# Context attention in a four-layer decoder: the rows of the next sequence are normed one group of heads before the group that transposes them

## The chip, the cores and the metric

The kernel runs on one core of one Trainium2 chip. The metric is the device time of one execution in microseconds (us), read as the median of several runs. The engines are TensorE (PE, its weight loads as PEld), VectorE (DVE), ScalarE (ACT), GpSimd (POOL) and SyncE (SP), each with its own stream of instructions that it works off in order.

## What is computed

A decoder of four layers on x, 8 sequences of 112 rows of 256 numbers, with a context of 8 x 375 rows of 128 numbers. Each layer is an attention, an attention over the context ("xattn") and a feed-forward part, each added to x after a layer norm of its input. The change touches three of these parts. The one of layer 3 is the shortest:

```python
x = x + _L3_xattn_ref(_layernorm(x, axis=-1), ctx_512, L3_xattn_Wq, L3_xattn_Wkv, L3_xattn_Wo)

def _L3_xattn_ref(x, z, Wq, Wkv, Wo):
    Q = (x @ Wq.T).reshape(B, xN, NUM_HEADS, HEAD_DIM)          # 16 heads of 16
    KV = (z @ Wkv.T).reshape(B, zN, 2, NUM_HEADS, HEAD_DIM)
    attn = softmax(einsum('bqhd,bkhd->bhqk', Q, K) * SCALE)
    O = einsum('bhqk,bkhd->bqhd', attn, V).reshape(B, xN, DIM)
    return O @ Wo.T
```

Layer 1's is the same with biases. Layer 2's second block (`a2_...` weights) has 16 heads of 32, norms its input twice, norms the context too, and has a GELU part behind it.

## The kernel before

`build` runs twelve stages one after the other, and a stage opens only when all engines have closed the one before. The three stages of the change are `Cross(k, "l1x")` (layer 1, about 788 to 957 us of the profile), `L2Block2` (about 1456 to 1667 us) and `CrossL3` (about 2080 to 2252 us), all of the class `Tiled` (L828).

**One order for all engines.** `Tiled.order` (L856) yields steps (kind, sequence b, index), and every engine's function walks through the same list and issues its own share of each step. So a step's place in the list sets its place in the stream of every engine that has a share in it. A sequence's 16 heads go in four groups of four, g = 0 to 3. Iteration (b, g) yields, in this order:

- `four` of the next group: 4 score products on PE, one into each of the banks 0 to 3 (L908); DVE takes the row maxima in two halves (L994). PE waits first until all four exponentials of the group before have left the banks (L905);
- `turn4` (g, 0), then `low` and `high` of the next group (ACT, 4 exponentials with their sums, L956), then `turn4` (g, 1): PE transposes the weights of this group (L917, by the helper at L264), ACT copies the first third (L978) and DVE the two others (L1002);
- `values4` of the group before (PE, L934), `turn4` (g, 2);
- then the list `plan[g]`: small steps for the sequence b + ahead. `stats` is a chain of four instructions on DVE (`bn_stats` L785, memset L787, `bn_aggr` L788, L790), with one power on POOL (L811) for the inverse deviation; `xn` is DVE's subtract and multiply of the 112 x 256 rows (L795), which waits for that power; `xT` is two transposes on PE (L548, by L264), which wait for `xn`, and DVE's copy (L798; L2231 in layer 2); `q`, `k`, `v`, `vv` are the projections (PE by L259), `inverse` the transposed reciprocal sums (PE, and ACT L984), `y` the output projection;
- after group 0, `norm` of the sequence before (DVE L1015).

In layer 2 `plan[0]` goes on behind `xT` with `cstat` (DVE, statistics of the context, L2378 to L2386), `v` 2 and `cn` (POOL, L2398 and L2405), and the context's transpose `cT` in group 1 waits for `cn`. There `ln` and `xm` make the rows that `xn` reads.

There is one buffer `xn`, one `xT` and one set of row statistics, `k.stats`. Transposes and projections take their banks in turn from a ring of three (4, 5, 7); a product waits until the bank's last reader is done (`fill`, L243). The context of each sequence comes by a DMA on SP's queue.

Of the kernel before, what the change touches and what calls it, by code (L numbers as in the profile page):

```python
# [827 lines left out]
class Tiled(Attention):  # L828
# [11 lines left out]
    second = ()  # L840
# [1047 lines left out]
class Cross(Tiled):  # L1888
# [1 line left out]
    hd = 16  # L1890
    scale, k_pieces, qm = 0.25, KD, None
    prologue = (("stats", 0), ("xn", 0), ("k", 0), ("xT", 0), ("parity", 0), ("q", 0))
    second = (("k", 1, 0), ("vv", 0, 0), ("v", 2, 0), ("stats", 0, 1))
    plan = ((("inverse", 0, -1), ("xn", 0, 1), ("xT", 0, 1)),
            (("q", 0, 1), ("k", 0, 1)),
            (("y", 0, -1), ("k", 1, 1)),
            (("vv", 0, 1), ("stats", 0, 2), ("v", 2, 1)))
    epilogue = (("y", 0),)

    def __init__(self, k, pack):  # L1900
# [72 lines left out]
class L1Attn(TiledSelf):  # L1973
# [3 lines left out]
    second = (("v", 0, 0), ("stats", 0, 1), ("xn", 0, 1), ("xT", 0, 1))  # L1977
    plan = ((("k", 0, 1),), (("q", 0, 1), ("near", 0, 0)), (("v", 0, 1), ("stats", 0, 2)), (("xn", 0, 2),),
            (("xT", 0, 2), ("y", 0, 0)))
# [304 lines left out]
class L2Block1(L2Block, TiledSelf):  # L2284
    k_pieces, key_step, v_by_act = 1, 4, (0,)
    lib, ln, ln3 = 4, 0, 8
    prologue = (("ln", 0), ("xm", 0), ("stats", 0), ("xn", 0), ("xT", 0), ("k", 0), ("q", 0))
    second = (("v", 0, 0), ("ln", 0, 1), ("xm", 0, 1), ("stats", 0, 1), ("xn", 0, 1), ("xT", 0, 1))
    plan = ((("k", 0, 1), ("xn3", 0, -1), ("ln", 0, 2)), (("q", 0, 1), ("xm", 0, 2)),
            (("v", 0, 1), ("xT3", 0, -1), ("stats", 0, 2)), (("xn", 0, 2),), (("xT", 0, 2), ("y", 0, 0), ("stats3", 0, 0)))  # L2290
# [27 lines left out]
class L2Block2(L2Block, Tiled):  # L2318
    k_pieces, v_by_act = 4, (0, 1, 2)
    lib, ln, ln3 = 6, 2, 16  # L2320
    prologue = (("ln", 0), ("xm", 0), ("cstat", 0), ("stats", 0), ("cn", 0), ("xn", 0), ("xT", 0), ("q", 0), ("cT", 0),
                ("k", 0), ("k", 1))
    second = (("k", 2, 0), ("v", 0, 0), ("v", 1, 0), ("ln", 0, 1), ("xm", 0, 1), ("stats", 0, 1))
    plan = ((("inverse", 0, -1), ("xn", 0, 1), ("xT", 0, 1), ("cstat", 0, 1), ("v", 2, 0), ("cn", 0, 1)),
# [3 lines left out]
    epilogue = (("y", 0), ("stats3", 0), ("xn3", 0), ("xT3", 0))  # L2328

    def __init__(self, k):  # L2330
# [1352 lines left out]
```

## Time and profile before

| what | value |
|---|---|
| median of 3 runs (lowest, highest) | 2377.60 us (2376.21, 2378.54) |
| span of the profiled execution | 2376.3 us |
| busy: PE, DVE, ACT, POOL | 2041.1, 1355.0, 884.5, 502.1 us |
| PE's share of the chain of waits that ended last | 66% |
| mean clock granted to PE | 0.857 of full speed |

The profile is one execution, and for that one only the span, first to last instruction, is given; it lies inside the three runs, 1.3 us below their median. Busy times are of the whole program; the three stages of the change take about a quarter of it. In a timeline a row gives the start, the duration, the engine, the line, what is written and read, how many instructions are merged, and in brackets the idle time before it with the one that ended it. "End" below is start plus duration.

### The profile page before, as it was taken

What the parts mean: (1) busy time and instruction counts of PE and PEld (TensorE: products, weight loads), DVE (VectorE), ACT (ScalarE), POOL (GpSimd) and SP (SyncE); (2) the same over time, 40 slices, a digit from 0 to 9 for tenths busy, and PEclk for the clock granted to TensorE, in tenths of its full rate; (3) what the DMA queues carried; (4) which work ended last, traced back from release to release, by engine and by line L of the source; (5) the groups of instructions that cost most, each with busy time, mean ns of one, the idle gap of its engine ahead of it and who ended that gap; (6) DMA issues with size and microseconds to landing.
All of it is one profiled execution on the core that took longest, in us unless ns stands there. A gap on an engine that the chain in (4) does not pass through costs nothing.

```text
span 2376.3 us, 57229 instructions
## 1 busy us (share of the span) xinstructions
PE 2041.1 (86%) x22720; PEld 1482.7 (62%) x22720; DVE 1355.0 (57%) x3605; ACT 884.5 (37%) x3421; POOL 502.1 (21%) x1131
## 2 busy tenths in 40 slices
PE   7999999998978799897977887999999998889843
PEld 3788888786656566466865654666554544556522
DVE  5666666674345688544634723787263210678797
ACT  2344444353236566211324522665111111246511
POOL 3344444221001100101324512332000000401111
PEclk9655555799988899998998998999899999789956
DMA  3000000104000000300021000000030000000000
GB/s 133 4 5 4 5 4 5 74 2 177 1 1 1 14 11 5 133 1 23 1 80 47 2 1 10 8 8 5 1 147 0 1 0 1 1 14 15 2 0 16
DMA packets 7752, 57.20 MB, mean 24 GB/s; under 512 B 760, under 2 KB 5216, under 8 KB 5728
## 3 DMA queue, kind: packets, MB, share of 16 engines
q1 hardware_dynamic: 7488, 53.54, 5.9%
q8 instruction: 183, 3.00, 0.5%
q14 instruction: 81, 0.66, 0.1%
HBM read 52.62 MB, written 0.92 MB: 23 GB/s over the span
## 4 chain that ended last, share of the span: by engine, by line
PE 66%; DVE 16%; issue 9%; ACT 5%; POOL 4%; DMA 1%; DVEq 0%; POOLq 0%; ACTq 0%; SPq 0%
PE banks L259 42%; PE banks L264 8%; PE banks L1323 6%; PE banks L908 3%; DVE memory L1421 2%; PE banks L934 2%; ACT memory L1352 1%; PE banks L1474 1%; ACT memory L1359 1%; DVE memory L795 1%; DVE memory L1218 1%; DVE memory L1427 1%; DVE memory L1430 1%; DVE memory L1439 1%; DVE memory L994 1%
## 5 line engine op out<-in xcount | busy, mean ns | idle before, releaser
L259 PE MATMUL banks<-memory 128*112 128x256 f32 (+7 forms) x4192 | 1130.1, 426 | 68.9 <-POOL memory L2030 8.0
L259 PEld LDWEIGHTS banks<-memory 128*128 128x128 f32 (+3 forms) x4192 | 706.7, 196 | 396.3 <-issue 250.6
L264 PE MATMUL banks<-memory 112*125 112x112 f32 (+3 forms) x2000 | 309.8, 288 | 151.0 <-DVE memory L795 92.0
L264 PEld LDWEIGHTS banks<-memory 112*125 112x125 f32 (+3 forms) x2000 | 240.3, 173 | 270.0 <-issue 139.4
L1323 PE MATMUL banks<-memory 128*128 128x8 bf16 (+2 forms) x10752 | 325.8, 175 | 25.9 <-DVE memory L1439 5.8
L1323 PEld LDWEIGHTS banks<-memory 128*128 128x128 bf16 x10752 | 304.0, 104 | 48.3 <-DVE memory L1439 46.2
L956 ACT ACTIVATE memory<-banks,memory 112x375 f32<-112x375 f32 x384 | 215.4, 579 | 26.2 <-DVE memory L994 26.0
L994 DVE TENSOR_REDUCE memory<-banks 112x2 f32<-112x750 f32 x192 | 171.1, 934 | 45.4 <-PE banks L908 43.7
L1002 DVE COPY memory<-banks 125x448 f32<-125x448 f32 x192 | 116.6, 619 | 12.8 <-PE banks L264 8.7
L1421 DVE TENSOR_REDUCE memory<-banks 128x48 f32<-128x192 f32 x448 | 109.6, 286 | 5.5 <-PE banks L1323 5.5
L1502 ACT ACTIVATE memory<-memory 112x112 f32<-112x112 f32 x192 | 71.7, 375 | 86.2 <-DVE memory L1523 86.2
L811 POOL TENSOR_TENSOR memory<-memory 112x1 f32<-112x1 f32 x72 | 39.7, 551 | 299.2 <-DVE memory L790 297.7
L1352 ACT ACTIVATE memory<-memory 128x48 f32<-128x48 f32 x224 | 54.4, 243 | 128.0 <-DVE memory L1421 128.0
L978 ACT COPY memory<-banks 125x448 f32<-125x448 f32 x96 | 51.1, 533 | 130.6 <-PE banks L264 130.6
L908 PE MATMUL banks<-memory 32*112 32x375 f32 x768 | 89.0, 533 | 8.6 <-ACT memory L956 6.3
L3142 DVE TENSOR_TENSOR memory<-banks,memory 112x256 f32<-112x256 f32 x8 | 3.4, 425 | 158.4 <-PE banks L259 158.4
L1383 POOL TENSOR_TENSOR memory<-memory 128x16 f32<-128x16 f32 x224 | 48.6, 217 | 205.7 <-DVE memory L1439 205.7
L1201 ACT ACTIVATE memory<-banks,memory 112x112 f32<-112x112 f32 x256 | 86.4, 391 | 9.7 <-DVE memory L1218 8.2
L1366 ACT COPY banks<-memory 128x48 f32<-128x48 f32 x448 | 79.8, 178 | 23.7 <-DVE memory L1400 23.7
L3119 ACT ACTIVATE memory<-banks,memory 128x448 f32<-128x448 f32 x32 | 20.3, 635 | 173.5 <-PE banks L259 173.5
L1439 DVE SCALAR_TENSOR_TENSOR memory<-memory 128x16 f32<-128x16 f32 x224 | 39.2, 175 | 75.7 <-ACT memory L1359 75.7
L956 ACT ACTIVATION_READ_ACCUMULATOR memory<-banks,memory 112x1 f32 x384 | 80.6, 210 | 0.0
(233 smaller groups left out, 2404.1 us busy)
## 6 DMA issues: line engine op xcount, KB each, us to landing
memory<-in_l2x SPq DMA_DIRECT2D x1, 7680.0 KB, 21.5
memory<-in_l2f SPq DMA_DIRECT2D x1, 7168.0 KB, 19.6
memory<-in_l1f SPq DMA_DIRECT2D x1, 4617.0 KB, 15.9
memory<-in_ctxT SPq DMA_DIRECT2D x24, 187.5 KB
memory<-in_l0a SPq DMA_DIRECT2D x1, 4224.0 KB, 16.1
memory<-in_l2f SPq DMA_DIRECT2D x1, 4096.0 KB, 12.9
memory<-in_l3f SPq DMA_DIRECT2D x1, 3073.0 KB, 22.4
memory<-in_l2a SPq DMA_DIRECT2D x1, 3072.0 KB, 19.2
```

Of the source, the lines that this page charges most:

```text
L259: ins = self.nc.tensor.matmul(out, weights[i], acts[i], start=i == 0, stop=i == n - 1)
L264: return self.nc.tensor.transpose(out, in_, self.ident[0:n, 0:n])
L908: ins = PE.matmul(k.bank(bank, S, CK), q, kT, start=True, stop=True)
L956: self.nc.scalar.activation(self.P_both[gi % 2][:, r, :], self.k.bank(r, S, CK), ACT.Exp, bias=u["nmax"][:, 4 * i + r:4 * i + r + 1], scal ...
L994: V.tensor_reduce(u["nmax"][:, 4 * i + 2 * h:4 * i + 2 * h + 2], k.banks[0:S, 2 * h:2 * h + 2, 0:CK], AX, ALU.max, negate=True).then_inc(* ...
L1002: V.tensor_copy(self.PT_both[gi % 2][0:CR, c, :], k.bank(k.at["turn", gi, c], CR, 4 * S)).then_inc(*s.pt_v.up())
L1201: A.activation(self.P_all[:, i, g, :], k.bank(i, S, 4 * S)[:, g * S:(g + 1) * S], ACT.Exp, bias=u["nmax"][:, 4 * i + g:4 * i + g + 1], sca ...
L1323: ins = self.nc.tensor.matmul(own[:, part:3, at:at + B], whh[:, part, l, j, g * P:(g + 1) * P], self.upper[l][:, 0:3 - part, j * B:(j + 1) ...
L1352: A.activation(self.gates[:, l, 1:4, :].rearrange("p g c -> p (g c)"), self.sums[:, l, 0:6 * B], ACT.Tanh).then_inc(*s.act_tanh.up())
L1366: self.nc.scalar.copy(self.slots[l][last][:, 3, :], src).then_inc(*self.s.xw_in.up())
L1421: V.tensor_reduce(self.sums[:, l, first * B:end * B], self.slots[l][last].rearrange("p s c -> p c s"), AX, ALU.add).then_inc(*s.gates_in.up())
L1502: A.activation(weights, weights, ACT.Exp, bias=self.nmax[n % 2][:, at:at + 1], scale=1.0, accum_out=self.total[n % 2][:, at:at + 1]).then_ ...
```

## The change

Two tables are rewritten, the `plan` and `second` of `Cross` (which `CrossL3` inherits) and of `L2Block2`. In `Cross`, `stats` of sequence b + 2 moves from group 3 to the end of group 2 of iteration b, and `xn` of the same sequence from group 0 of the next sequence to the end of group 3, behind `v`. In `L2Block2` `stats` stays and `xn` moves in the same way, behind `xT3` and `v` 1. In `second`, the steps between the first two groups of scores, `xn` of sequence 1 is put last, and in `Cross` `stats` of sequence 1 is put ahead of the value projections. Nothing is added or taken out.

```diff
 class Cross(Tiled):
-    second = (("k", 1, 0), ("vv", 0, 0), ("v", 2, 0), ("stats", 0, 1))
-    plan = ((("inverse", 0, -1), ("xn", 0, 1), ("xT", 0, 1)),
+    second = (("k", 1, 0), ("stats", 0, 1), ("vv", 0, 0), ("v", 2, 0), ("xn", 0, 1))
+    plan = ((("inverse", 0, -1), ("xT", 0, 1)),
             (("q", 0, 1), ("k", 0, 1)),
-            (("y", 0, -1), ("k", 1, 1)),
-            (("vv", 0, 1), ("stats", 0, 2), ("v", 2, 1)))
+            (("y", 0, -1), ("k", 1, 1), ("stats", 0, 2)),
+            (("vv", 0, 1), ("v", 2, 1), ("xn", 0, 2)))
 class L2Block2(L2Block, Tiled):
-    second = (("k", 2, 0), ("v", 0, 0), ("v", 1, 0), ("ln", 0, 1), ("xm", 0, 1), ("stats", 0, 1))
+    second = (("k", 2, 0), ("v", 0, 0), ("v", 1, 0), ("ln", 0, 1), ("xm", 0, 1), ("stats", 0, 1), ("xn", 0, 1))
-    plan = ((("inverse", 0, -1), ("xn", 0, 1), ("xT", 0, 1), ("cstat", 0, 1), ("v", 2, 0), ("cn", 0, 1)),
+    plan = ((("inverse", 0, -1), ("xT", 0, 1), ("cstat", 0, 1), ("v", 2, 0), ("cn", 0, 1)),
...
-            (("k", 2, 1), ("xn3", 0, -1), ("v", 0, 1), ("stats", 0, 2), ("xT3", 0, -1), ("v", 1, 1)))
+            (("k", 2, 1), ("xn3", 0, -1), ("v", 0, 1), ("stats", 0, 2), ("xT3", 0, -1), ("v", 1, 1), ("xn", 0, 2)))
```

The instructions of PE, ACT and SP keep their order; only DVE's and POOL's streams differ. This is DVE's in layer 1, from the output addition of a sequence (L779, L781, group 2) to the copy of the next sequence's turned rows (L798, group 0). Before:

```order
1546 L779 TENSOR_TENSOR memory<-banks,memory 112x256
1547 L781 TENSOR_TENSOR memory<-memory 112x256
1548 L994 TENSOR_REDUCE memory<-banks 112x2 x2
1549 L1002 COPY memory<-banks 125x448 x2
1550 L1007 RECIPROCAL memory<-memory 112x16
1551 L1094 TENSOR_TENSOR memory<-banks,memory 125x2x8x16 x2
1552 L785 BN_STATS memory<-memory 112x6
...
1556 L1080 TENSOR_TENSOR memory<-banks,memory 125x8x16 x2
1557 L994 TENSOR_REDUCE memory<-banks 112x2 x2
1558 L1002 COPY memory<-banks 125x448 x2
1559 L795 TENSOR_SCALAR memory<-memory 112x256
1560 L798 COPY memory<-banks 128x224
```

After:

```order
1546 L779 TENSOR_TENSOR memory<-banks,memory 112x256
1547 L781 TENSOR_TENSOR memory<-memory 112x256
1548 L785 BN_STATS memory<-memory 112x6
...
1552 L994 TENSOR_REDUCE memory<-banks 112x2 x2
1553 L1002 COPY memory<-banks 125x448 x2
1554 L1007 RECIPROCAL memory<-memory 112x16
1555 L1094 TENSOR_TENSOR memory<-banks,memory 125x2x8x16 x2
1556 L1080 TENSOR_TENSOR memory<-banks,memory 125x8x16 x2
1557 L795 TENSOR_SCALAR memory<-memory 112x256
1558 L994 TENSOR_REDUCE memory<-banks 112x2 x2
1559 L1002 COPY memory<-banks 125x448 x2
1560 L798 COPY memory<-banks 128x224
```

The four instructions of `stats` stand one group earlier, ahead of the maxima of the next sequence's group 0; the norm L795 stands ahead of the maxima of group 1 and of two copies, where it stood behind them. Layer 3 has the same order with other lines. In layer 2, on DVE, from the end of group 3 into group 0, this is the difference (minus is before, plus is the change; L2231 is first the copy of `xT3`, then that of `xT`):

```order
 L790 TENSOR_SCALAR memory<-memory 112x1
 L2231 TENSOR_SCALAR memory<-banks,memory 128x112 x2
-L994 TENSOR_REDUCE memory<-banks 112x2 x2
-L1002 COPY memory<-banks 125x448 x2
-L795 TENSOR_SCALAR memory<-memory 112x256
+L795 TENSOR_SCALAR memory<-memory 112x256
+L994 TENSOR_REDUCE memory<-banks 112x2 x2
+L1002 COPY memory<-banks 125x448 x2
 L2231 TENSOR_SCALAR memory<-banks,memory 128x112 x2
 L2378 BN_STATS memory<-memory 125x6 x3
```

Here only the norm moves, ahead of two maxima and two copies. On POOL, the power L811 of layers 1 and 3 now stands ahead of the copy L1034 (`share`) in each sequence, where it stood behind it; in layer 2 POOL's order is as before.

## Rows read from the trace of the kernel before

**Rows 1.** Who waited for whom, PE, whole span: total, times, longest.

```profile
PE banks L264 <- DVE memory L795: 92.0, 39, 9.9
```

**Rows 2.** PE's transposes (L264): idle before them ended by L795; layers 1, 2, 3.

```profile
  DVE memory L795: 9.8, 7
...
  DVE memory L795: 9.2, 8
...
  DVE memory L795: 9.9, 8
```

**Rows 3.** Timeline, layer 1, group 3 into group 0 of a middle sequence.

```profile
840.12 0.42 DVE L785 BATCH_NORM_STATS2 memory<-memory 112x6 f32<-112x256 f32 x1
...
840.87 0.49 DVE L1080 TENSOR_TENSOR memory<-banks,memory 125x128 f32<-125x128 f32 x2
...
841.27 1.77 DVE L994 TENSOR_REDUCE memory<-banks 112x2 f32<-112x750 f32 x2
...
842.24 0.57 ACT L956 ACTIVATE memory<-banks,memory 112x375 f32<-112x375 f32 x1 [0.38 <-DVE memory L994]
842.36 0.88 PE L264 MATMUL banks<-memory 112*125 112x112 f32 x6
...
844.02 0.41 DVE L795 TENSOR_SCALAR memory<-memory 112x256 f32<-112x256 f32 x1
844.35 0.21 ACT L956 ACTIVATION_READ_ACCUMULATOR memory<-banks,memory 112x1 f32 x1
...
844.48 0.41 PE L264 MATMUL banks<-memory 112*128 112x112 f32 x2 [1.24 <-DVE memory L795]
...
844.82 0.90 PE L908 MATMUL banks<-memory 32*112 32x375 f32 x8
```

**Rows 4.** The same timeline later: groups 1 to 3, scores and maxima.

```profile
849.58 0.90 PE L908 MATMUL banks<-memory 32*112 32x375 f32 x8
...
850.51 1.78 DVE L994 TENSOR_REDUCE memory<-banks 112x2 f32<-112x750 f32 x2 [0.66 <-PE banks L908]
...
855.22 1.78 DVE L994 TENSOR_REDUCE memory<-banks 112x2 f32<-112x750 f32 x2 [0.57 <-PE banks L908]
...
858.39 0.22 ACT L956 ACTIVATION_READ_ACCUMULATOR memory<-banks,memory 112x1 f32 x1
...
858.81 0.90 PE L908 MATMUL banks<-memory 32*112 32x375 f32 x8
```

**Rows 5.** Timeline, layer 3: maxima behind the output addition, and PE's wait.

```profile
2152.02 1.78 DVE L994 TENSOR_REDUCE memory<-banks 112x2 f32<-112x750 f32 x2 [1.04 <-PE banks L908]
...
2160.33 0.41 PE L264 MATMUL banks<-memory 112*128 112x112 f32 x2 [1.24 <-DVE memory L795]
```

**Rows 6.** Timeline, layer 2: group 3 into groups 0 and 1 of a middle sequence.

```profile
1520.96 0.55 POOL L811 TENSOR_TENSOR memory<-memory 112x1 f32<-112x1 f32 x1 [0.93 <-DVE memory L790]
...
1522.07 1.78 DVE L994 TENSOR_REDUCE memory<-banks 112x2 f32<-112x750 f32 x2 [0.58 <-PE banks L908]
...
1525.39 0.41 PE L264 MATMUL banks<-memory 112*128 112x112 f32 x2 [0.66 <-DVE memory L795]
...
1525.84 0.70 DVE L2231 TENSOR_SCALAR memory<-banks,memory 128x112 f32<-128x112 f32 x2 [0.51 <-PE banks L264]
...
1528.16 1.77 DVE L994 TENSOR_REDUCE memory<-banks 112x2 f32<-112x750 f32 x2
...
1531.14 0.54 PE L264 MATMUL banks<-memory 125*128 125x125 f32 x3 [0.60 <-POOL memory L2405]
```

**Rows 7.** Timeline, layer 2, first sequence: PE's longest wait for the norm.

```profile
1476.08 0.63 PE L264 MATMUL banks<-memory 112*128 112x112 f32 x2 [4.14 <-DVE memory L795]
```

**Rows 8.** Windows, layer 1: PE, PEld, DVE, ACT, POOL busy, granted clock, DMA share, GB/s.

```profile
900.00:902.00 2.00, 0.76 (x10) 0.41 (x9) 1.58 (x4) 1.96 (x8) 0.00 (x0) 1.00 0.19 68
902.00:904.00 2.00, 2.00 (x12) 0.93 (x12) 1.23 (x3) 0.00 (x0) 0.00 (x0) 0.54 0.00 0
```

**Rows 9.** Timeline, layer 1: `share` copies, one in each sequence.

```profile
877.51 0.40 POOL L1034 COPY memory<-memory 112x256 f32<-112x256 f32 x1 [16.90 <-DVE memory L1007]
896.56 0.40 POOL L1034 COPY memory<-memory 112x256 f32<-112x256 f32 x1 [16.89 <-DVE memory L1007]
917.19 0.40 POOL L1034 COPY memory<-memory 112x256 f32<-112x256 f32 x1 [18.47 <-DVE memory L1007]
```

**Rows 10.** Timeline, layer 3's prologue: a norm beside POOL's memsets.

```profile
2085.00 2.75 DVE L795 TENSOR_SCALAR memory<-memory 112x256 f32<-112x256 f32 x1 [0.73 <-POOL memory L811]
```

**Rows 11.** Windows as in rows 8: first sequences of layers 1, 3 and 2.

```profile
807.00:809.00 2.00, 2.00 (x29) 1.66 (x28) 1.66 (x3) 1.82 (x6) 0.00 (x0) 0.50 0.00 0
...
2104.00:2106.00 2.00, 2.00 (x28) 1.47 (x28) 1.47 (x3) 2.00 (x8) 0.00 (x0) 0.50 0.00 0
...
1476.00:1478.00 2.00, 1.92 (x4) 0.79 (x4) 1.27 (x6) 0.16 (x2) 0.00 (x0) 0.50 0.00 0
```

**Rows 12.** Timeline, layer 2: POOL's norm of the context.

```profile
1528.73 2.36 POOL L2405 TENSOR_SCALAR memory<-memory 125x128 f32<-125x128 f32 x3
```

**Rows 13.** Timeline, layer 1: `share` of the sequence of rows 3.

```profile
839.41 0.40 POOL L1034 COPY memory<-memory 112x256 f32<-112x256 f32 x1 [16.89 <-DVE memory L1007]
```

## The prediction

> **What bounds the kernel now.** I began with the list of who waited for whom on PE, since PE is busy 86% of the span and has two thirds of the chain that ended last. Its first line is the wait of the transposes (L264) for the norm L795: 92.0 us in 39 waits [rows 1]. That sum is of the whole program. Cut to the three stages that the change touches, it is 9.8, 9.2 and 9.9 us [rows 2], 28.9 us in all, and a few of these 23 waits stand in the prologues, which the change leaves alone. So the gain cannot reach 29 us, and most of the 92 us lie in stages without an edit.
>
> Next the timeline of a middle sequence of layer 1, to see what would end PE's idle time if the norm were there. PE is done with the last turn and the inverse at 842.36 + 0.88 = 843.24, stands 1.24 us, transposes the rows at 844.48 and starts the scores at 844.82 [rows 3]. But the scores have a second condition: the last exponential of the group before must have left its bank. It ends at 844.35 + 0.21 = 844.56 [rows 3], and where this condition alone held PE, PE began 0.20 us later (858.39 + 0.22 = 858.61, then 858.81) [rows 4]. So with the norm for nothing, the scores could start at 844.76 instead of 844.82. **The wait of 1.24 us hides another that ends 0.06 us earlier.** The exponentials began at 842.24, released by the maxima, and these began at 841.27 with no idle time before them: DVE was late [rows 3]. PE alone would let the maxima start 0.93 us after the scores, as at 849.58 and 850.51 [rows 4]. What the change is worth in layers 1 and 3 is therefore what it does to DVE's place of the maxima of group 1, not to the norm.
>
> **The change, part by part.**
>
> *Layer 1, a middle sequence (6 of them).* Out of the stretch ahead of the group 1 maxima goes `stats`, 840.87 - 840.12 = 0.75 us [rows 3]. In comes the norm, 0.41 us [rows 3]. An instruction of DVE can start a little before the one ahead has ended (L1080 ends at 840.87 + 0.49 = 841.36, the maxima start at 841.27 [rows 3]), so that 0.32 to 0.41 us of it count; I take 0.37. The maxima start 0.38 us earlier. The 0.75 us of `stats` go to the end of group 2, where DVE idles 0.57 us before the maxima of group 0 [rows 4]. So these start about 0.11 to 0.18 us later, and DVE has no idle time from there to the maxima of group 1. Net 0.20 to 0.27 us earlier; exponentials and the next scores follow by the same amount. The transposes themselves stop waiting for the norm: they now wait for DVE's first copy of the group, which frees their bank, and for nothing behind it. I take **0.25 us a sequence**, times 6 is 1.5 us. The bounds are 0.06 (the maxima do not move) and 1.24 (PE's whole wait).
>
> *Layer 3 (6 middle sequences).* PE's wait is the same 1.24 us, but the output addition is one instruction instead of two, and DVE idles 1.04 us before the group 0 maxima [rows 5]. That covers the 0.75 us of `stats` wholly; if this cover were gone, the case would be layer 1's. The full 0.38 us arrives, plus up to 0.06 of the hidden slack: **0.40 us**, times 6 is 2.4 us.
>
> *Layer 2 (6 middle sequences).* Here only the norm moves. It stands behind the power L811, which ends at 1520.96 + 0.55 = 1521.51 [rows 6], so it runs from about 1521.55 to 1521.95, and the maxima of group 1 began at 1522.07 after 0.58 us of idle time [rows 6]. It is covered, with 0.1 us to spare. In group 0 PE waited 0.66 us at the transposes [rows 6]; without it the rows' copy on DVE comes 0.65 us earlier than 1525.84, and behind it, with no gap, the context's statistics, `norm` and the maxima of group 2 at 1528.16 [rows 6]. So DVE's chain moves by the full amount, and with it POOL's `cn`, for which PE waits 0.60 us at 1531.14 [rows 6]: that wait stays, but ends earlier. I take **0.64 us**, times 6 is 3.8 us. The bounds are 0 (another wait takes all of it) and 0.66.
>
> *The first sequence of each stage.* In layers 1 and 3 `stats` of sequence 1 moves into time in which DVE waits for the value projections, and costs nothing; the norm takes its place ahead of the maxima. By the same 0.38 us the scores of group 2 come earlier: 0.8 us for both. In layer 2 DVE is held in `second` by the norm's wait for POOL's power (0.55 us) before it may take the maxima, a loss of about 1.1 us, but PE's wait of 4.14 us [rows 7] shrinks by more. I take a gain of 0.5 us, between -1 and +2.
>
> PE, ACT and SP keep their order, and the DMA of the context waits for the same steps as before. POOL's power now stands ahead of `share`, which waits for DVE much longer than the power takes: nothing. The sum is 1.5 + 2.4 + 3.8 + 0.8 + 0.5 = **9.0 us**.
>
> *The clock.* At 902 us the granted clock falls from 1.00 to 0.54 behind a window in which PE was busy 0.76 of 2 us [rows 8], that is to the lower of its levels of 2.4 and 1.2 GHz. The engine had just stood its 1.24 us. That sequence took 917.19 - 896.56 = 20.63 us, the one before 896.56 - 877.51 = 19.05 [rows 9], so the fall cost 1.58 us. One of six like waits brought it on; with the gap cut in two I expect none there. That gives 1.6 us, **10.6 us in all**. The first sequences of all three stages have such a stretch at the lower level too (0.50 from 807, from 2104 and from 1476 us) [rows 11], and I leave those as they are. The Trainium skill (TensorE: Matmul & The Clock Gate, Part 1) says that the monitor behind the clock runs freely and does not start with the kernel. By this rule a gap may or may not bring a fall, and the sum would stay at 9.0 us on average; the trace agrees so far that one of six like gaps did it.
>
> Against the profiled span this is 2376.3 - 10.6 = 2365.7 us. The span is 1.3 us under the median of the three runs, so for the median I predict 2377.6 - 10.6 = **2367 us**. A measurement of this kernel can tell about 0.2%, 4.8 us, from no change.
>
> **The rivals.**
>
> *The hidden wait keeps nearly all.* If the maxima of group 1 do not come earlier in layers 1 and 3, each of 14 sequences gains 0.06 us, 0.8 us in all. With layer 2's 4.3 us and no clock gained the sum is 5 us: 2372.5 us, on the bound of no change. For it speaks that ACT idles only 0.38 us before its first exponential at 842.24 [rows 3]: its copy L978 is next in line there, and had that been any later, nothing would move; against it that 0.38 us of DVE's work leave the stretch for certain. Chance 0.13.
>
> *PE's whole wait goes.* All of the waits for the norm outside the prologues vanish, about 27 us: 2350 us. The exponentials' end at 844.56 speaks against it. Chance 0.03.
>
> *The clock gives more.* The falls in the three first sequences go too, each about 1.6 us, 5 us more: 2362 us. For it speaks that layer 2's follows right on the wait of 4.14 us for the norm [rows 7]; against it that PE still waits there for the exponentials. Chance 0.17.
>
> *Slower: DVE is held by the norm behind POOL.* DVE works in order, so while the norm waits for the power, the maxima, both copies and `xT`'s copy wait too. In layer 2 the power comes 0.1 us before the norm is due. If POOL were busy then with `cn` (2.36 us [rows 12]) or the chain behind `xm`, the maxima would be late by up to 2 us in each of 7 sequences, 14 us less the 9 of the gain: 2383 us. It decides from 0.6 us of lateness on, where layer 2 gives nothing. Against it: POOL had idled 0.93 us before that power [rows 6]. Akin to it is the port: one norm took 2.75 us instead of 0.41 beside POOL's memsets [rows 10]. The Trainium skill (SBUF — State Buffer, Who interferes with whom) says that VectorE in a two-port mode and GpSimd lock each other out for a whole instruction; the row agrees. It would add at most the 0.4 us of `share` in layers 1 and 3, 12 times, 4.8 us: 2372 us. But `share` runs from 839.41 to 839.81 [rows 13], and the norm's new place is near 840.5. Chance of both together 0.05.
>
> **How the numbers follow.** My forecast has the rest, 0.62. Its own range is 2363 to 2371: each of the 0.25, 0.40 and 0.64 may be off by half, 4 us. The range goes to the clock case below, with two more such falls gained or lost by chance in the later program (3 us and more), and to the hidden wait above: **2358 to 2374 us**. Faster by over 0.2% (under 2372.8 us) holds the forecast, the clock case, the whole wait and a part of the first rival: 0.85. Within 0.2%: 0.11. Slower: 0.04.
>
> **What would show it.** Right: PE's wait for L795 is gone from the middle sequences; in layer 1 and 3 PE idles instead about 0.6 us ahead of L908, put down to ACT L956; `share` comes every 18.8 and 18.65 us instead of 19.05; layer 2's are 0.64 us closer. Wrong: L994 of group 1 still 1.5 us behind the scores; an idle time of DVE ended by POOL L811 in layer 2 over 0.2 us; L795 longer than 0.5 us; or new falls of the clock in later stages that eat the gain.

## The result, and the profile after

The changed kernel takes **2362.6 us** (median of 4 runs, 2360.1 to 2364.5), the kernel before, measured beside it on the same chip, 2378.1 us (4 runs, 2376.2 to 2378.7). The ratio is 0.9933, interval 0.9921 to 0.9945: 15.4 us less. In a second comparison the same kernel gave 0.995, interval 0.9934 to 0.9966 (2364.5 against 2376.6 us). So the kernel is faster by 0.5 to 0.7%. The forecast was 2367 us with a range of 2358 to 2374: right side, inside the range, and a third too little.

The profiled executions differ by 2376.3 - 2363.2 = 13.1 us of span; the profiled one of the changed kernel is the slowest of its four, so that the trace accounts for 13.1 of the 15.4 us. The head of the changed kernel's page, its span, busy times and shares of the chain that ended last:

```profile
span 2363.2 us, 57229 instructions
...
PE 2043.6 (86%) x22720; PEld 1483.5 (63%) x22720; DVE 1354.9 (57%) x3605; ACT 883.8 (37%) x3421; POOL 500.9 (21%) x1131
...
PE 66%; DVE 14%; issue 9%; ACT 6%; POOL 4%; DMA 1%; DVEq 0%; POOLq 0%; ACTq 0%; SPq 0%
```

The work is the same: as many instructions, PE as busy. Less of the chain now goes through DVE (14%, 16% before). Who waited for whom on PE, whole program, changed kernel (us in total, times, longest), answers to [rows 1]:

```profile
PE banks L264 <- DVE memory L795: 66.7, 19, 9.9
...
PE banks L908 <- ACT memory L956: 17.4, 21, 1.9
```

92.0 - 66.7 = 25.3 us of waits for the norm are gone, yet the span is only 13.1 us shorter. The second line tells the rest: PE now stands before the scores, waiting for the exponentials (before, this line was 6.3 us in 7 waits). This is the hidden wait of the prediction. A middle sequence of layer 1 shows it, in the timeline of the changed kernel (start, duration, engine, line, [idle before <- what ended it]); it answers to [rows 3]:

```profile
839.06 0.40 POOL L1034 COPY memory<-memory 112x256 f32<-112x256 f32 x1 [2.44 <-DVE memory L1007]
...
839.41 0.90 PE L908 MATMUL banks<-memory 32*112 32x375 f32 x8
...
840.16 0.40 DVE L795 TENSOR_SCALAR memory<-memory 112x256 f32<-112x256 f32 x1
...
840.48 1.77 DVE L994 TENSOR_REDUCE memory<-banks 112x2 f32<-112x750 f32 x2
...
842.01 1.30 PE L264 MATMUL banks<-memory 112*125 112x112 f32 x8
...
842.17 1.19 DVE L1002 COPY memory<-banks 125x448 f32<-125x448 f32 x2
...
842.90 0.20 PEld L264 LDWEIGHTS banks<-memory 112*128 112x128 f32 x2 [0.22 <-issue]
...
843.56 0.21 ACT L956 ACTIVATION_READ_ACCUMULATOR memory<-banks,memory 112x1 f32 x1
...
843.92 0.90 PE L908 MATMUL banks<-memory 32*112 32x375 f32 x8 [0.61 <-ACT memory L956]
...
848.68 0.90 PE L908 MATMUL banks<-memory 32*112 32x375 f32 x8
...
853.39 0.90 PE L908 MATMUL banks<-memory 32*112 32x375 f32 x8
...
857.56 0.40 POOL L1034 COPY memory<-memory 112x256 f32<-112x256 f32 x1 [2.43 <-DVE memory L1007]
```

The six transposes of the last turn and of the inverse and the two of the rows are now one row of eight (842.01), and PE no longer waits for the norm there. From scores to scores it is 4.51, 4.76 and 4.71 us here. Before, the same three intervals were 5.05, 4.76 and 4.71, by these starts of the scores in the timeline of the kernel before:

```profile
839.77 0.90 PE L908 MATMUL banks<-memory 32*112 32x375 f32 x8
...
844.82 0.90 PE L908 MATMUL banks<-memory 32*112 32x375 f32 x8
...
854.29 0.90 PE L908 MATMUL banks<-memory 32*112 32x375 f32 x8
```

(849.58 stands in [rows 4].) The fourth interval is 4.52 us in both (853.39 to 857.91 now, 854.29 to 858.81 before). So **one interval of the four changed, by 0.54 us**: the one in which PE had waited 1.24 us. `share` comes every 857.56 - 839.06 = 18.50 us instead of 19.05 [rows 9, 13]. In layer 3 it is the same, 2162.88 - 2144.38 = 18.50; the changed kernel's timeline:

```profile
2144.38 0.40 POOL L1034 COPY memory<-memory 112x256 f32<-112x256 f32 x1 [2.88 <-DVE memory L1007]
...
2149.24 0.90 PE L908 MATMUL banks<-memory 32*112 32x375 f32 x8 [0.61 <-ACT memory L956]
...
2162.88 0.40 POOL L1034 COPY memory<-memory 112x256 f32<-112x256 f32 x1 [2.88 <-DVE memory L1007]
```

Layer 2, timeline of the changed kernel, answers to [rows 6]:

```profile
1516.04 0.64 POOL L1034 COPY memory<-memory 112x512 f32<-112x512 f32 x1 [3.40 <-DVE memory L1007]
...
1517.71 0.90 PE L908 MATMUL banks<-memory 32*112 32x375 f32 x8
...
1518.26 0.41 DVE L795 TENSOR_SCALAR memory<-memory 112x256 f32<-112x256 f32 x1
...
1518.65 1.78 DVE L994 TENSOR_REDUCE memory<-banks 112x2 f32<-112x750 f32 x2
...
1520.31 1.26 PE L264 MATMUL banks<-memory 112*125 112x112 f32 x10
...
1521.62 0.70 DVE L2231 TENSOR_SCALAR memory<-banks,memory 128x112 f32<-128x112 f32 x2
...
1522.83 0.90 PE L908 MATMUL banks<-memory 32*112 32x375 f32 x8
...
1526.91 0.54 PE L264 MATMUL banks<-memory 125*128 125x125 f32 x3
...
1539.60 0.64 POOL L1034 COPY memory<-memory 112x512 f32<-112x512 f32 x1 [3.40 <-DVE memory L1007]
```

The norm starts at 1518.26, right after POOL's power, and the maxima follow without a gap. `share` comes 1539.60 - 1516.04 = 23.56 us apart, where it was 24.45. On average over the six middle sequences it is 23.54 against 24.40, since the first of them is shorter in both.

**Where the 13.1 us of span come from**, from `share` to `share` or from scores to `share` in both traces. The middle sequences: layer 1 took 820.36 to 936.24 (115.88 us) and takes 820.57 to 931.56 (110.99), 4.9 us less: 6 x 0.55 = 3.3, and 1.6 for the fall of the clock at 902 that is gone. Layer 2 went from 146.41 to 141.25, 5.2 us less. Layer 3 went from 114.31 to 110.99, 3.3 us less. First sequences: 0.5 in layer 1, 0.6 in layer 3, 0.0 in layer 2. That is 14.5 us. The other 1.4 us were lost outside the three stages, where no line was changed: 0.7 ahead of layer 1 and 2.1 between it and layer 2 (a lead of 4.7 us at 936 is 2.6 at layer 2's first scores), with 1.4 gained between layers 2 and 3. In the windows between layers 1 and 2 the granted clock was 0.92 before and 0.91 after, us, busy time of PE, PEld, DVE, ACT and POOL, clock; changed kernel:

```profile
821.00:932.00 111.00, 107.11 (x1216) 75.25 (x1216) 96.97 (x190) 74.96 (x234) 5.13 (x11) 1.00 0.04 10
...
953.00:1457.00 504.00, 423.94 (x2582) 314.63 (x2583) 237.64 (x626) 147.12 (x529) 136.10 (x163) 0.91 0.09 34
```

That the stretch between shifted because the clock's falls landed elsewhere fits these two figures, but is argued and not shown. The first line shows layer 1 at the full level throughout.

### The profile page after: what moved, and what is told of

Same layout as the page of the kernel before. It is cut to its first block, busy times and chain, and to the rows that moved or that the text cites. A ratio compares the mean times of both kernels' runs of the same rounds, so it can differ in the third digit from the quotient of the medians.

```text
span 2363.2 us, 57229 instructions
## 1 busy us (share of the span) xinstructions
PE 2043.6 (86%) x22720; PEld 1483.5 (63%) x22720; DVE 1354.9 (57%) x3605; ACT 883.8 (37%) x3421; POOL 500.9 (21%) x1131
## 4 chain that ended last, share of the span: by engine, by line
PE 66%; DVE 14%; issue 9%; ACT 6%; POOL 4%; DMA 1%; DVEq 0%; POOLq 0%; ACTq 0%; SPq 0%
PE banks L259 42%; PE banks L264 8%; PE banks L1323 6%; PE banks L908 3%; ACT memory L956 2%; DVE memory L1421 2%; PE banks L934 2%; ACT memory L1352 1%; PE banks L1474 1%; ACT memory L1359 1%; DVE memory L1218 1%; DVE memory L795 1%; DVE memory L1427 1%; DVE memory L1430 1%; DVE memory L1439 1%
## 5 line engine op out<-in xcount | busy, mean ns | idle before, releaser
L264 PE MATMUL banks<-memory 112*125 112x112 f32 (+3 forms) x2000 | 305.9, 286 | 123.7 <-DVE memory L795 66.7
L264 PEld LDWEIGHTS banks<-memory 112*125 112x125 f32 (+3 forms) x2000 | 238.6, 172 | 240.3 <-issue 142.9
L956 ACT ACTIVATE memory<-banks,memory 112x375 f32<-112x375 f32 x384 | 215.4, 579 | 19.5 <-DVE memory L994 19.1
L811 POOL TENSOR_TENSOR memory<-memory 112x1 f32<-112x1 f32 x72 | 39.6, 550 | 416.1 <-DVE memory L790 414.6
L1002 DVE COPY memory<-banks 125x448 f32<-125x448 f32 x192 | 116.8, 619 | 11.3 <-PE banks L264 6.9
L908 PE MATMUL banks<-memory 32*112 32x375 f32 x768 | 88.4, 529 | 19.6 <-ACT memory L956 17.4
L956 ACT ACTIVATION_READ_ACCUMULATOR memory<-banks,memory 112x1 f32 x384 | 80.4, 209 | 0.0
```

The costliest lines, as they stand in the source:

```text
L264: return self.nc.tensor.transpose(out, in_, self.ident[0:n, 0:n])
L908: ins = PE.matmul(k.bank(bank, S, CK), q, kT, start=True, stop=True)
L956: self.nc.scalar.activation(self.P_both[gi % 2][:, r, :], self.k.bank(r, S, CK), ACT.Exp, bias=u["nmax"][:, 4 * i + r:4 * i + r + 1], scal ...
L1002: V.tensor_copy(self.PT_both[gi % 2][0:CR, c, :], k.bank(k.at["turn", gi, c], CR, 4 * S)).then_inc(*s.pt_v.up())
```

## Experiments

Two theories stood against each other. A: what counts in layers 1 and 3 is how long DVE works between the scores of group 1 and their maxima. B: the wait of PE for the norm is what counts. The change moves both; the experiments move them one at a time. The first four ran beside the kernel before at 2378.9 us (median of 14 runs), the others at 2376.6 us (11 runs).

### The norm alone moved (layers 1 and 3)

```
-    second = (("k", 1, 0), ("vv", 0, 0), ("v", 2, 0), ("stats", 0, 1))
-    plan = ((("inverse", 0, -1), ("xn", 0, 1), ("xT", 0, 1)),
+    second = (("k", 1, 0), ("vv", 0, 0), ("v", 2, 0), ("stats", 0, 1), ("xn", 0, 1))
+    plan = ((("inverse", 0, -1), ("xT", 0, 1)),
...
-            (("vv", 0, 1), ("stats", 0, 2), ("v", 2, 1)))
+            (("vv", 0, 1), ("stats", 0, 2), ("v", 2, 1), ("xn", 0, 2)))
```

`stats` stays in group 3; layer 2 is as before.

> Layers 1 and 3 only: the norm of sequence b + 2 moves to the end of group 3, but the statistics stay in group 3 between vv and v. Layer 2 is as before the change. Theory A (what counts is when DVE reaches the maxima of group 1): DVE now does statistics, wait for POOL's power and norm ahead of them, so they start about 0.6 us later than before (0.33 us of norm and some 0.3 us of waiting for L811), the exponentials and the next scores with them: 19.5 to 19.7 us a sequence by the spacing of L1034 instead of 19.05, and 2382 to 2385 us. PE waits for ACT L956 about 1.2 us ahead of the scores of group 2. Theory B (what counts is PE's wait for the norm, which is gone here as in the changed kernel): 18.5 us a sequence as there, and about 2369 us.

Measured: 2412.8 us (4 runs, 2410.6 to 2419.7), ratio 1.0135, interval 1.0119 to 1.0152: **34 us slower**. From the timeline of this kernel, layer 1:

```profile
846.24 0.90 PE L908 MATMUL banks<-memory 32*112 32x375 f32 x8
...
847.49 0.55 POOL L811 TENSOR_TENSOR memory<-memory 112x1 f32<-112x1 f32 x1 [1.21 <-DVE memory L790]
...
848.07 0.41 DVE L795 TENSOR_SCALAR memory<-memory 112x256 f32<-112x256 f32 x1 [0.25 <-POOL memory L811]
...
848.40 1.78 DVE L994 TENSOR_REDUCE memory<-banks 112x2 f32<-112x750 f32 x2
...
850.86 0.38 PE L264 MATMUL banks<-memory 112*128 112x112 f32 x2 [1.15 <-DVE memory L1002]
...
851.84 0.90 PE L908 MATMUL banks<-memory 32*112 32x375 f32 x8 [0.60 <-ACT memory L956]
```

PE's wait for the norm is gone here as well, and the interval is 851.84 - 846.24 = 5.60 us, 0.55 longer than before. PE still stands before the transposes, though: they now wait 1.15 us for DVE's first copy L1002, as the prediction said of the change (the bank of the transposes is the one that this copy empties). In the list of who waited for whom of this kernel, whole program, that is

```profile
PE banks L264 <- DVE memory L1002: 13.8, 12, 1.2
```

one wait in each of the twelve middle sequences of layers 1 and 3. With `stats`, the power's 0.25 us and the norm ahead of them, the maxima start 2.16 us behind the scores instead of 1.50. B is refuted as it was stated: the wait for L795 can go and the kernel be slower. What this run shows is that the maxima's place sets both of PE's waits, the one for L1002 before the transposes and the one for the exponentials behind them. A's spacing of 19.5 to 19.7 us is 19.05 + 0.55 = 19.60. But the measured spacing is 21.15 (`share` at 845.88, 867.03, 888.18), and that is a second thing. The next interval, without an edit, took 6.30 us instead of 4.76, and the windows of this kernel show why (clock is the third figure from the end):

```profile
850.00:852.00 2.00, 0.54 (x6) 0.39 (x10) 1.63 (x4) 1.93 (x8) 0.00 (x0) 1.00 0.00 0
852.00:854.00 2.00, 2.00 (x15) 1.46 (x15) 1.63 (x3) 0.33 (x1) 0.00 (x0) 0.73 0.00 0
854.00:856.00 2.00, 2.00 (x28) 1.48 (x27) 1.13 (x2) 2.00 (x8) 0.00 (x0) 0.50 0.00 0
```

PE was busy 0.54 of the 2 us, and the granted clock fell from its upper level, 2.4 GHz, to its lower, 1.2 GHz. Here that cost 1.54 us. Of the twelve middle sequences of layers 1 and 3 eight take 21.2 us and four 22.6, none 19.6. Against 19.05 that is 8 x 2.1 + 4 x 3.6 = 31 of the 34 us. The expectation had the direction and the mechanism, and missed this price, which is three times that of the delay of 0.55 us itself.

### The statistics alone moved (layers 1 and 3)

```
-    second = (("k", 1, 0), ("vv", 0, 0), ("v", 2, 0), ("stats", 0, 1))
+    second = (("k", 1, 0), ("stats", 0, 1), ("vv", 0, 0), ("v", 2, 0))
...
-            (("y", 0, -1), ("k", 1, 1)),
-            (("vv", 0, 1), ("stats", 0, 2), ("v", 2, 1)))
+            (("y", 0, -1), ("k", 1, 1), ("stats", 0, 2)),
+            (("vv", 0, 1), ("v", 2, 1)))
```

The norm stays in group 0, layer 2 as before.

> Layers 1 and 3 only: the statistics move to the end of group 2, the norm stays in group 0 as before, and PE still waits for it. Layer 2 is as before the change. Theory A: the 0.75 us of statistics leave the stretch ahead of the maxima of group 1 and nothing comes in, so maxima, copies and the norm come 0.7 us earlier; the transposes wait for the norm until about 4.1 us behind the scores of group 1, which is no later than the exponentials allow. 18.5 to 18.6 us a sequence, nearly the changed kernel's 18.50 without moving the norm, 2368 to 2371 us. Theory B: the norm stands where it did and PE waits for it, so 19.05 us a sequence stays, 2376 to 2379 us.

Measured: 2370.0 us (4 runs), ratio 0.9958, interval 0.9943 to 0.9974. Spacing 18.66 us (`share` at 839.33, 857.99), the same in layer 3. So 0.39 of the 0.55 us come **without the norm being moved at all** (the expectation was 18.5 to 18.6). The time itself says less than the spacing: 12 x 0.39 = 4.7 us of the 8.9. In this trace the first sequences of both layers have no fall of the clock (their interval to the scores of group 3 is 4.75 us, before 6.31), and there is none at 902; that is 3.1 and 1.6 us by the trace, not by this edit alone. Timeline of this kernel:

```profile
839.68 0.90 PE L908 MATMUL banks<-memory 32*112 32x375 f32 x8
...
840.62 1.78 DVE L994 TENSOR_REDUCE memory<-banks 112x2 f32<-112x750 f32 x2
...
843.54 0.40 DVE L795 TENSOR_SCALAR memory<-memory 112x256 f32<-112x256 f32 x1
...
844.00 0.20 PEld L264 LDWEIGHTS banks<-memory 112*128 112x128 f32 x2 [1.06 <-DVE memory L795]
```

The maxima start 0.94 us behind the scores, sooner than in the changed kernel (1.07), yet the interval is 4.67 us (next scores at 844.35), not 4.51. The norm ends at 843.94 and the transposes start at 844.00. The row of their weight load puts the wait down to the norm; the row of the transposes themselves names ACT L956, whose last exponential ends at 843.99, but `xT` has no wait for ACT among its steps. So in this kernel the norm does hold PE, and its move is worth the 4.67 - 4.51 = 0.16 us that the changed kernel has over it.

### Each layer alone

Only layer 2's two tables changed (first), and only those of layers 1 and 3 (second), each as in the diff of the change.

> Only layer 2's second block has its edit; layers 1 and 3 are as before the change. If the gains add, layer 2 gives 24.45 - 23.56 = 0.89 us in each of six middle sequences, 5.3 us, and its first sequence about nothing: 2372 us, give or take 2 us of clock falls elsewhere. If the gain of the changed kernel came from falls of the clock that the shift of the program undid, the spacing of L1034 in layer 2 would stay at 24.45 us and the time at 2377 us.

> Only layers 1 and 3 have their edit; layer 2 is as before the change. Theory A: 18.50 us a sequence in both, 12 x 0.55 = 6.6 us, about 1 us for the first sequences and 1.6 us if the fall of the clock at 902 us is gone: 2368 to 2370 us. With layer 2's 5.3 us this is the whole 15.4 us within 2 us. If layers 1 and 3 gave no more than forecast (0.25 and 0.40 us a sequence), the spacing would be 18.80 and 18.65 us.

Measured: layer 2 alone 2373.9 us (10 runs), ratio 0.9982, interval 0.9971 to 0.9994; layers 1 and 3 alone 2368.3 us (5 runs), 0.9956, interval 0.9942 to 0.997. The spacings go with the edits: 23.56 in layer 2 and 19.05 elsewhere in the first, 18.50 and 24.43 in the second. One of the 19.05 is an exception: in layer 3 of the first a sequence took 22.26 us, and in the windows of its trace the clock falls from 1.00 to 0.54 behind the stretch 2172 to 2174, where PE was busy 1.12 of 2 us and had stood its 1.24 us. That is a second fall like the one at 902, and it cost 3.2 us. 0.18% and 0.44% add up to 0.62%, between the 0.5 and 0.67% of the two comparisons of the whole change. The spacings show no action of the parts on one another; the times could not show a small one. By the spacings layer 2 should have had 5.3 us of the 2378.9, 0.22%; that lies within its interval.

### The key projection earlier, the layer norm's rows earlier, and both

The changed kernel leaves PE idle 0.61 us per sequence in layers 1 and 3 and gains nothing in layer 2's first sequence. The first of these edits is to fill the idle time, the second lets POOL's power of sequence 1 come sooner.

```
+    plan = ((("inverse", 0, -1), ("xT", 0, 1), ("k", 0, 1)),
+            (("q", 0, 1),),
```

```
-    second = (("k", 2, 0), ("v", 0, 0), ("v", 1, 0), ("ln", 0, 1), ("xm", 0, 1), ("stats", 0, 1), ("xn", 0, 1))
+    second = (("ln", 0, 1), ("xm", 0, 1), ("k", 2, 0), ("v", 0, 0), ("v", 1, 0), ("stats", 0, 1), ("xn", 0, 1))
```

> The changed kernel, and in layers 1 and 3 the first key projection of the next sequence moves from group 1's list to the end of group 0's, into the 0.61 us in which PE waits for the exponentials ahead of the scores of group 2. Theory A: of the four intervals from scores to scores (4.51, 4.76, 4.71, 4.52 us) the first becomes about 4.6, the second falls to the 4.51 of the ring scores, maxima, exponentials, scores: 18.3 to 18.4 us a sequence instead of 18.50, some 2 us in all. If PE's wait is not usable (the projection itself waits for its bank or its copy holds ACT back), the spacing stays at 18.50 or grows.

> The changed kernel, and in layer 2's second block the first norm of sequence 1 (ln and xm) comes first in the list between the first two groups of scores. DVE's wait for POOL's chain ahead of the maxima of group 1 of sequence 0 shrinks: they start about 0.9 us earlier relative to the scores of group 0. The six middle sequences stay at 23.56 us. About 1 us in all, too little for the time to show.

> The changed kernel with the edits of the two runs before together. 18.3 to 18.4 us a sequence in layers 1 and 3, 23.56 in layer 2, and 3 us less than the changed kernel, 2359 to 2361 us, if the granted clock is as there.

> The changed kernel as it is, once more on this chip, so that the run before can be read against it: 2361 to 2365 us, 18.50, 23.56 and 18.50 us a sequence.

Measured in a single run each: 2360.3 us for the first, 2360.6 for the second. Both together, 6 runs: 2360.1 us (2357.8 to 2366.3), ratio 0.9935, interval 0.9919 to 0.9951, and the changed kernel itself beside them 2364.5 us, 0.995, interval 0.9934 to 0.9966. The intervals overlap, so no better version is shown. The traces do say where the 4.4 us between the two medians may lie: the middle sequences cost 12 x 0.09 = 1.1 us more, but from its first scores to its `share` the first sequence takes 22.79, 28.23 and 22.84 us in layers 1, 2 and 3 with both edits, and 24.69, 30.08 and 24.72 in the changed kernel beside it, 5.6 us less. Part of that is falls of the clock that this trace does not have (see below), and one trace of each cannot tell the edit's share from chance.

**The first expectation was wrong.** The spacing is 18.59 us instead of 18.50 or less. Timeline of that kernel:

```profile
843.23 0.87 PE L259 MATMUL banks<-memory 128*128 128x375 f32 x2 [0.20 <-DVE memory L1002]
...
844.03 0.90 PE L908 MATMUL banks<-memory 32*112 32x375 f32 x8
...
848.49 0.90 PE L908 MATMUL banks<-memory 32*112 32x375 f32 x8 [0.28 <-ACT memory L956]
```

PE is free, but the projection waits 0.20 us for a bank that DVE's copy L1002 has to empty, and, being 0.87 us long, ends after the exponentials have (844.10 against 843.48). The scores start 4.90 us behind those before (839.13) instead of 4.51, and of the 0.39 us lost the next interval gives back 0.30 (4.46 for 4.76). Even without the wait for the bank the projection would have been longer than the 0.61 us of idle time; the wait added 0.20 to that.

**The second came out as expected, and is too small to be seen in the time.** From the first to the third scores of layer 2, changed kernel run again:

```profile
1464.39 0.90 PE L908 MATMUL banks<-memory 32*112 32x375 f32 x8
...
1477.57 1.61 PE L908 MATMUL banks<-memory 32*112 32x375 f32 x8
```

and with both edits:

```profile
1462.91 0.90 PE L908 MATMUL banks<-memory 32*112 32x375 f32 x8
...
1475.16 1.60 PE L908 MATMUL banks<-memory 32*112 32x375 f32 x8
```

13.18 against 12.25 us, 0.9 us won, once in the program. The middle sequences stay at 23.56.

## Why the prediction was right, and where it was off

**The reading was right.** PE's wait for the norm hid the wait for the exponentials, which came next as said: 0.61 us ahead of L908, put down to ACT L956, `share` closer. That DVE's place of the maxima decides, and not the norm, is shown by both halves of the edit: without `stats` moved the wait for the norm vanishes (one of 1.15 us for L1002 takes its place) and 0.55 us are lost; without the norm moved 0.39 of 0.55 us are won. The forecast sum for layers 1 to 3 was 1.5 + 3.8 + 2.4 = 7.7 us for the middle sequences; it is 3.3 + 5.2 + 3.3 = 11.8.

**Layer 1, 0.25 us forecast, 0.55 measured.** Three terms were mis-sized. (1) The step "the maxima of group 0 start 0.11 to 0.18 us later, and DVE has no idle time from there to the maxima of group 1" was wrong. They start 1.02 us behind the scores instead of 0.93, but the two copies L1002 behind them take it up: their row is 1.23 us long instead of 1.31, and the reciprocal L1007 starts 3.86 us behind the scores in both kernels (857.25 - 853.39, before 858.15 - 854.29). A row of two merged copies hides a short wait of the second one; 1.14 to 1.19 us are enough elsewhere. The value addition L1094 in turn starts 0.32 us ahead of the next scores in the changed kernel (839.09, 839.41) and 0.33 before (839.44, 839.77). I subtracted a delay of 0.13 us that nothing carried on. (2) The norm costs 0.32 us from its start to the maxima's, 840.48 - 840.16, not 0.37, the lower end of what the rows gave. With both, the maxima come 0.43 us earlier relative to the scores (1.07 for 1.50), which is 0.75 - 0.32. (3) The hidden slack, which the term of layer 1 left out, was 0.11 us, not 0.06: the exponentials take 3.29 us from the maxima's start in both kernels, and the scores follow their end after 0.26 us before, after 0.15 now (843.77, 843.92). I had taken 0.20 from one row of another group. 0.43 + 0.11 = 0.54, the change of the interval; in the terms of the forecast 0.25 + 0.13 + 0.05 + 0.11.

**Layer 3, 0.40 forecast, 0.55 measured.** Only (2) and (3) apply; the two layers run in the same ring (scores, maxima, exponentials, scores), and once nothing else holds it, it takes the same 18.50 us in both.

**Layer 2, 0.64 forecast, 0.88 measured.** That DVE's chain moves by the whole amount was right: group 0's interval gained 0.42 (5.12 for 5.54) and group 1's 0.46 (6.27 for 6.73). The amount was too small, since I priced only the wait of 0.66 us. The two transposes themselves took 0.41 us alone [rows 6]. In the stream of ten they add 1.26 - 1.07 = 0.19. Together the rows' copy L2231 comes 0.86 us earlier behind the scores (1521.62 - 1517.71 = 3.91, before 1525.84 - 1521.07 = 4.77). The wait of 0.60 us for `cn`, which I had kept, shrank to 0.15 (1526.76 to 1526.91). Not all of PE's 0.66 us went: the projection behind the transposes now waits 0.23 us for the bank that DVE's copy L1002 has to empty.

**First sequences.** 0.8 us for layers 1 and 3 was about right (0.5 + 0.6). Layer 2's 0.5 was wrong, it is 0.0. The loss was the one priced at about 1.1 us: DVE stood for POOL's power, here 0.66 us, with the maxima behind it, and these start 4.37 us behind the scores instead of 3.31. Changed kernel, timeline of layer 2's start, answers to [rows 7]:

```profile
1470.40 0.55 POOL L811 TENSOR_TENSOR memory<-memory 112x1 f32<-112x1 f32 x1 [0.23 <-DVE memory L790]
...
1470.98 0.41 DVE L795 TENSOR_SCALAR memory<-memory 112x256 f32<-112x256 f32 x1 [0.66 <-POOL memory L811]
1471.31 1.77 DVE L994 TENSOR_REDUCE memory<-banks 112x2 f32<-112x750 f32 x2
1471.45 0.41 PE L264 MATMUL banks<-memory 112*128 112x112 f32 x2 [2.12 <-DVE memory L795]
...
1473.77 2.04 PE L259 MATMUL banks<-memory 128*125 128x512 f32 x2 [1.90 <-DVE memory L1002]
```

PE's wait for the norm shrank from 4.14 to 2.12 us, and the step that failed was to count this as gained: right behind it the value projection now waits 1.90 us for the bank that L1002, late with the maxima, has to empty. Together that is 4.02 us.

**The transposes** were said to wait for DVE's first copy, which frees their bank. In layers 1 and 3 they do: the first of the two copies L1002 alone runs from 842.17 to 842.78, and the weight load of the transposes starts at 842.90 behind 0.22 us of idle time. The same 0.12 us lie between this copy's end and the transposes in layer 3 (2148.10, 2148.22) and in the kernel with only the norm moved, where the view names L1002. It changed no term, as the scores wait for ACT anyway.

**The clock.** The fall at 902 is gone, 1.58 us, as forecast. In one pair of traces that could be chance, since one such wait in twelve had brought it on. All traces together bear it out: of the 24 middle sequences of layers 1 and 3 with the wait of 1.24 us (the kernel before, and the one with only layer 2 changed) two had a fall, of the 84 in the seven traces with a shorter wait (the statistics alone, layers 1 and 3 alone, and all kernels with the whole change) none. In the changed kernel's trace the first sequences kept theirs, so the rival with 5 us more from them did not happen; 2362 us was reached by the sizes of the steps instead. But whether the first sequences of layers 1 and 3 have a fall ahead of the scores of group 3 changes from trace to trace. The interval that shows it, about 6.3 us with a fall, is 4.5 to 4.8 in both layers with the statistics alone moved and in both kernels with the key projection earlier, and in layer 3 alone of three more. What decides it stays open; some 1.5 us for each of these intervals in a single trace should not be put down to an edit. The slower rival, DVE held behind POOL, happened once in the program at 0.66 us, and nowhere in the middle sequences, where the power was done in time. The sum of what was edited would be 14.5 us in the trace; 1.4 us of it went elsewhere between the stages.

## What to carry to other kernels

When an engine waits for X, look at what else it needs at that place and when that is ready: the gain is the distance to the next condition, then whatever moves that one. Here moving the late instruction alone, the obvious edit, put 0.66 us more in front of the maxima and cost 34 us; it had to be paid for by taking something longer out of the same stretch. An instruction priced by its row's duration is a bound only: in a stream behind its like, where nothing holds it, it can cost half of that. And idle time can be filled only by something shorter, and if a bank is free at that moment as well: here the wait for a bank took up most of what layer 2's first sequence should have gained.

## What the runs showed of the hardware that was not expected

- **Waits of PE can cost a multiple of their length.** In layer 1, the granted clock fell behind waits of 1.15 and 0.60 us close together in the kernel with only the norm moved (mean clock 0.89 over 814 to 920, before 0.98), 1.54 us in the sequence read; by the spacings none of the twelve sequences was spared. The single wait of 1.24 us had a fall behind it in two of 24 sequences (1.58 and 3.2 us), that of 0.61 us in none of 48. The Trainium skill (TensorE: Matmul & The Clock Gate, Why this matters for your kernels) advises against idle gaps between bursts of matmuls, and the gaps that it warns of are longer than these. In the middle sequences no gap was longer than 1.24 us, and the clock fell all the same.
- **Two transposes cost 0.19 us behind eight others and 0.41 us alone** (1.26 and 1.07 us for ten and eight in layer 2). In layer 1, where they wait for their bank, they cost 0.42 us behind six others (1.30 and 0.88 us for eight and six).
- **The norm of 0.40 us delays DVE's next instruction by 0.32 us** (840.16 to 840.48): the reduce behind it starts before it has ended.
